# Units 3 and 4 moved between P times u and the grams, and the output turn one pair of units later

## What is computed

```python
xn = _layernorm(x, axis=-1)
x = x + _L0_attn_ref(xn, ...) + _L0_ffn_ref(xn, ...)
# attention: q, k, v through a causal convolution of 4 taps and silu, beta and g from xn
def step(S, inp):
    q_t, k_t, v_t, g_t, b_t = inp
    S = S * jnp.exp(g_t)[..., None, None]
    mem = jnp.einsum('bhk,bhkv->bhv', k_t, S)
    delta = (v_t - mem) * b_t[..., None]
    S = S + jnp.einsum('bhk,bhv->bhkv', k_t, delta)
    o_t = jnp.einsum('bhk,bhkv->bhv', q_t, S)
    return (S, o_t)
...
o = o * jax.lax.rsqrt(jnp.mean(o * o, axis=-1, keepdims=True) + eps)
o = o * jax.nn.silu(g_out.reshape(Bm, Tm, H, DV))
return o.reshape(Bm, Tm, VAL_DIM) @ o_w.T
# feed-forward, I = 1408
gate_up = jnp.einsum('bsh,oh->bso', x, w_gu)
gate, up = (gate_up[..., :I], gate_up[..., I:])
h = jax.nn.silu(gate) * up
y = jnp.einsum('bsi,hi->bsh', h, w_down)
rms = jnp.sqrt(jnp.mean(y * y, axis=-1, keepdims=True) + EPS)
return y / rms
```

## Time and profile before

| | |
|---|---|
| median of 3 runs | 3232.68 us (3232.13 to 3233.97) |
| the profiled execution | 3249.4 us, span 3247.6 us |
| PE busy, share of the span | 3114.7 us, 96% |
| DVE busy | 2489.0 us, 77% |
| POOL busy | 1912.5 us, 59% |
| ACT busy | 1664.1 us, 51% |
| DMA, mean busy share of 16 engines, stretch of the loop | 0.06 |

### The profile page before, as it was taken

How to read it: one execution, slowest core, us unless ns; L and a number is a source line. 1 busy time by engine, 2 the same in 40 slices (tenths; PEclk the granted TensorE clock), 3 DMA queues, 4 the chain that set the end, 5 groups by cost and what they waited for, 6 DMA issues and landing times.

```text
span 3247.6 us, 117622 instructions
## 1 busy us (share of the span) xinstructions
PE 3114.7 (96%) x45504; PEld 2207.2 (68%) x45504; DVE 2489.0 (77%) x5509; ACT 1664.1 (51%) x3336; POOL 1912.5 (59%) x2955
## 2 busy tenths in 40 slices
PE   5999999999999999999999999999999999999987
PEld 4676776766766766766767767667667666667664
DVE  7777777877777777777777777777777777777763
ACT  4544555544555545555445555445555455554452
POOL 4566555666555665556665556665556665566642
PEclk8999999999999999999999999999999999999997
DMA  3000000000000000000000000000000000000000
GB/s 121 8 21 19 8 18 21 21 21 15 9 21 21 21 21 5 18 22 21 21 19 8 18 21 21 21 15 9 21 21 21 21 5 18 22 21 21 15 3 21
DMA packets 34301, 64.95 MB, mean 20 GB/s; under 512 B 5360, under 2 KB 7152, under 8 KB 33776
## 3 DMA queue, kind: packets, MB, share of 16 engines
q1 hardware_dynamic: 29808, 52.13, 5.0%
q10 hardware_dynamic: 4096, 6.42, 0.6%
HBM read 41.76 MB, written 16.78 MB: 18 GB/s over the span
## 4 chain that ended last, share of the span: by engine, by line
PE 78%; DVE 14%; issue 5%; POOL 2%; ACT 0%; DVEq 0%; DMA 0%; SPq 0%; POOLq 0%; ACTq 0%
PE PS L1220 14%; PE PS L1176 14%; PE PS L1207 8%; PE PS L1208 7%; PE PS L1432 7%; PE PS L1292 6%; DVE arena L912 5%; PE PS L1275 3%; PE PS L1357 3%; DVE arena L1012 2%; PE PS L1310 2%; PE PS L1410 2%; PE PS L1328 2%; DVE arena L384 2%; PE PS L1232 1%
## 5 line engine op out<-in xcount | busy, mean ns | idle before, releaser
L912 DVE SCALAR_TENSOR_TENSOR arena<-PS,sc,arena 128x256 f32<-128x256 f32 x2112 | 1000.7, 480 | 358.6 <-ACT arena L606 236.5
L1207 PE MATMUL PS<-xh,wgu 128*128 128x256 f32 x2816 | 901.4, 352 | 15.1 <-DVE arena L912 10.6
L1208 PE MATMUL PS<-xl,wgu 128*128 128x256 f32 x2816 | 700.7, 281 | 0.0
L606 ACT ACTIVATE arena<-PS,sc 128x256 f32<-128x256 f32 x704 | 329.8, 473 | 708.0 <-PE PS L1208 704.0
L1220 PE MATMUL PS<-wdn,inner 128*128 128x512 f32 x1408 | 656.3, 592 | 0.0
L1207 PEld LDWEIGHTS PS<-xh,wgu 128*128 128x128 f32 x2816 | 530.9, 189 | 146.8 <-issue 76.3
L503 POOL TENSOR_TENSOR work<-arena 128x31 f32<-128x31 f32 (+15 forms) x992 | 521.4, 526 | 141.0 <-DVE arena L1012 65.8
L1208 PEld LDWEIGHTS PS<-xl,wgu 128*128 128x128 f32 x2816 | 531.6, 189 | 97.3 <-issue 97.1
L507 POOL TENSOR_TENSOR arena<-arena,work 128x31 f32<-128x31 f32 (+15 forms) x992 | 543.1, 547 | 77.9 <-POOL work L503 0.2
L1176 PE MATMUL PS<-xnT,wqkv 128*128 128x256 f32 x2048 | 490.2, 391 | 9.0 <-ACT inner L586 9.0
L1176 PEld LDWEIGHTS PS<-xnT,wqkv 128*128 128x128 f32 x2048 | 382.5, 193 | 75.3 <-issue 13.6
(11 more groups left out here) (160 smaller groups left out, 4665.2 us busy)
## 6 DMA issues: line engine op xcount, KB each, us to landing
xt<-in_x SPq DMA_DIRECT2D x64, 256.0 KB, 3.4
obuf<-in_x SPq DMA_DIRECT2D x64, 256.0 KB, 2.8
out<-obuf SPq DMA_DIRECT2D x64, 256.0 KB, 2.0
wqkv<-in_wqkv ACTq DMA_DIRECT2D x1, 2048.0 KB, 14.1
arena<-in_gup ACTq DMA_DIRECT2D x2, 704.0 KB, 6.4
arena<-in_dns SPq DMA_DIRECT2D x1, 1408.0 KB, 12.1
wg<-in_wg ACTq DMA_DIRECT2D x1, 1024.0 KB, 20.6
wo<-in_wo ACTq DMA_DIRECT2D x1, 1024.0 KB, 17.2
```

Source lines behind the costliest of these rows:

```text
L606: eng.activation(fa[:, u % 4, :], PS[:, bank(u, 0), 0:NB * P], ACT.Copy, scale=sc[:, u % 2, KB * m:KB * m + 1]).then_inc(fa_scaled.sem, 1)
L912: eng.scalar_tensor_tensor(out=fa[:, u % 4, :], in0=PS[:, bank(u, k // 2), k % 2 * NB * P:][:, 0:NB * P], scalar=sc[:, u % 2, KB * m + k:K ...
L1207: eng.matmul(o, w, xh[:, k, :], start=True, stop=False)
L1208: ins = eng.matmul(o, w, xl[:, k, :], start=False, stop=True)
```

## The change

On PE, units 3 and 4 and the last gate parts are written between the quarters of `p_times_u` and the two grams. Unit 5 and then the turns of v follow the second gram, and `down(0)` after them. Units up to 5 fill banks 5 and 4, where unit 4 filled 2 and 3; even units from 6 on fill 2 and 3. `turn_o` moves from behind unit 8 to behind unit 10, the four parts of `to_wo` from behind units 10 to 16 to behind units 12 to 18. ACT and DVE follow: DVE takes unit 3 and hidden(1) ahead of the reductions and unit 4 ahead of the gram products, ACT the silu of v ahead of unit 2. `result` and `layer_norm_apply` change places.

```diff
--- before.py
+++ after.py
@@ -358,7 +358,7 @@
 
         def bank(u, fill):
 
-            return 2 + fill if u >= 4 and u % 2 == 0 else 5 - fill
+            return 2 + fill if u >= 6 and u % 2 == 0 else 5 - fill
 
         def gate_bank(b):
             return 6 if b else 4
@@ -767,8 +767,13 @@
 
 
             unit(1)
+            if n:
+                eng.wait_ge(*taps_done.at(n, NQKV))
+                eng.activation(qkv[:, 4:NQKV, :], qkv[:, 4:NQKV, :], ACT.Silu).then_inc(silu_done.sem, 1)
+            unit(2)
             queries()
-            unit(2)
+            gate(1)
+            unit(3)
             if t:
                 eng.wait_ge(*pu_out.at(t, 1))
                 for b in range(NB):
@@ -786,18 +791,14 @@
                 eng.activation(ro[:, :, :], ro[:, :, :], ACT.Exp, scale=-0.5).then_inc(last_roots.sem, 1)
                 o_columns()
                 return
-            eng.wait_ge(*taps_done.at(n, NQKV))
-            eng.activation(qkv[:, 4:NQKV, :], qkv[:, 4:NQKV, :], ACT.Silu).then_inc(silu_done.sem, 1)
+            unit(4)
             gate_copy(1)
-            unit(3)
-            gate(1)
-            unit(4)
+            unit(5)
+            gate(2)
             for b in range(NB):
                 eng.wait_ge(*v_turned.at(n, b + 1))
                 eng.activation(R[:, b, :, 0:DV], PS[:, 6 + b, :].rearrange("p (h v) -> p h v", h=H),
                                ACT.Copy).then_inc(v_copied.sem, 1)
-            unit(5)
-            gate(2)
             if t:
                 eng.wait_ge(*o_gated.at(t, NB))
             eng.activation(gs[:, :, :], gsn[:, :, :], ACT.Silu).then_inc(gs_done.sem, 1)
@@ -807,7 +808,7 @@
                 unit(2 * m)
                 unit(2 * m + 1)
                 gate(m)
-                if m == 4:
+                if m == 5:
                     o_columns()
             if more:
                 x_transposed(eng, n.next(), n)
@@ -1087,6 +1088,8 @@
             unit(1)
             hidden(0)
             unit(2)
+            unit(3)
+            hidden(1)
             if t:
                 for b in range(NB):
                     eng.wait_ge(*osq_done.at(t, b + 1))
@@ -1094,10 +1097,9 @@
                                       ALU.add).then_inc(so_done.sem, 1)
                 if not n:
                     last_output()
+            unit(4)
             gram_products(0)
             gram_products(1)
-            unit(3)
-            hidden(1)
             if n:
                 turn_a(0)
             if not n:
@@ -1107,15 +1109,16 @@
 
 
             for m in range(2, FM):
-                unit(2 * m)
+                if m > 2:
+                    unit(2 * m)
                 unit(2 * m + 1)
                 hidden(m)
                 if m == 2:
                     turn_a(1)
-                if t and m in (6, 8):
-                    result((m - 6) // 2)
-                if more and m in (7, 9):
-                    layer_norm_apply(eng, n.next(), (m - 7) // 2)
+                if more and m in (6, 8):
+                    layer_norm_apply(eng, n.next(), (m - 6) // 2)
+                if t and m in (7, 9):
+                    result((m - 7) // 2)
             turn_t()
             eng.wait_ge(*res_loaded.at(n, 16 * NB))
             for i, b in enumerate((1, 0)):
@@ -1193,9 +1196,9 @@
                             eng.wait_ge(wgu_by_act.sem, 2)
                             eng.wait_ge(wgu_by_pool.sem, 2)
                             eng.wait_ge(wdn_done.sem, FM)
-                elif u <= 3:
+                elif u <= 5:
                     eng.wait_ge(*(fa_done if fill else fa_second).at(n, u))
-                elif u == 4:
+                elif u == 6:
                     if fill == 0:
                         eng.wait_ge(*p_done.at(n, NB))
                 else:
@@ -1505,20 +1508,23 @@
 
             half_unit(1, 0)
             gate(1, 0)
+            gate(1, 1)
             p_times_u(0)
             half_unit(1, 1)
             p_times_u(1)
+            half_unit(2, 0)
             turn_q()
-            gate(1, 1)
-            p_times_u(2)
-            half_unit(2, 0)
-            p_times_u(3)
             half_unit(2, 1)
             gate(1, 2)
+            p_times_u(2)
+            half_unit(3, 0)
+            p_times_u(3)
+            half_unit(3, 1)
+            gate(1, 3)
+            half_unit(4, 0)
             gram(0)
+            half_unit(4, 1)
             gram(1)
-            gate(1, 3)
-            unit(3)
             if not n:
                 turn_o()
                 for b in range(NB):
@@ -1527,23 +1533,22 @@
                 return
 
 
+            unit(5)
             for b in range(NB):
                 eng.wait_ge(*silu_done.at(n, NC + 1))
                 eng.wait_ge(*gate_copied.at(n, NB))
                 for m in range(4):
                     ins = eng.transpose(PS[:, 6 + b, m * P:(m + 1) * P], qkv[:, 4 + m, b * P:(b + 1) * P], ident[:, :])
                 ins.then_inc(v_turned.sem, 1)
-            unit(4)
-            unit(5)
             down(0)
             for i in range(6, NU):
                 unit(i)
                 if i % 2:
                     down((i - 5) // 2)
-                elif i == 8:
+                elif i == 10:
                     turn_o()
-                elif 10 <= i <= 16:
-                    to_wo((i - 10) // 4, (i - 10) // 2 % 2)
+                elif 12 <= i <= 18:
+                    to_wo((i - 12) // 4, (i - 12) // 2 % 2)
             down(9)
             if more:
                 transpose_x(eng, n.next(), t)
```

## The result

The changed kernel is slower: 3258.09 us (3253.97 to 3259.02, 4 runs) against 3233.32 (3232.13 to 3235.01, 4 runs) on one chip, ratio 1.0074, 95% interval 1.0061 to 1.0087. Forecast was 3198, faster, with a range of 3178 to 3222. The profiled execution took 3253.97 us; that of before, from which the prediction was worked, 3249.4.

A forecast was written before the change was run, and what follows sets the result against it. TensorE was taken as the bound. Fetch losses -1.39, waits -0.90-0.43, new waits +0.86+0.4, shifted starts +0.3 gave -1.1 us per iteration; with 0.15 more fetch, 31 steps gave -34, the first tile -1: 3232.7 to 3198, range 3178 to 3222.

The forecast's parts named there:

- The order on PE: From half_unit(1, 0) to the end of gram 1, the new TensorE order takes 13.74 us, bursts 0.68, half grams 1.02.
- the rows 128 apart: TensorE stops in bursts 128 rows (256 instructions) apart, awaiting instruction blocks available every 3.9 us; wide work between avoids most stops.
- The size of that term: Instruction-fetch losses at P times u and the grams: 1.55 us per iteration, nearly all expected to go, 0.15 kept.
- DVE is also held by unit 4, now ahead of them: On VectorE, unit 4 precedes the gram products; its last two steps end at 1065.2.
- So products start at 1065.25 and end at 1067.75: VectorE's gram products, which down(0) needs; TensorE, there at 1066.89, then waits 0.86 us.
- the reductions end 3.03 after the last burst: VectorE's reductions keep their old distance of 3.03 us behind the last P times u burst, so end at 1063.29.
- 0.86 at down(0): New TensorE wait of 0.86 us before down(0), for VectorE's gram products.
- 0.4 at unit 9: New TensorE wait of 0.4 us: unit 9's second half needs unit 7 done on VectorE.
- idle at unit 5: Sign of being wrong: TensorE idle at half_unit(4, 1) or unit 5, waiting on DVE.
- nothing for or against: After down(2), output turn and projection stand in pairs where DVE is level with PE: no gain or loss.
- The issue losses stay: Rival, chance 0.10: losses belong to the bursts, not to time since the last block; 3246 us, slower.
- the banks bite: Rival, chance 0.12: single banks and ScalarE's order make edges of units 3 to 5 miss, losing 0.5 us; 3214.

The follow-up runs named there:

- run 7: Kernel before with gate part 1 moved ahead of the first quarter of P times u on TensorE: 3236.22 us, ratio 1.0003.
- Run 5: Kernel before, unchanged, traced and timed again on one chip: 3235.16 us, ratio 0.9998.
- run 9: Changed kernel with one added wait: GpSimd starts its gate product only when hidden(1) is done: 3213.26 us, ratio 0.989.
- Run 1: Changed kernel with GpSimd's product of o with the gate on 8 of 512 columns only: 3229.53 us, ratio 0.9967.
- run 2: Changed kernel with hidden(1) moved behind the gram products on VectorE: 3213.9 us, ratio 0.9921.
- run 10: Kernel before with hidden(0) moved between the two reductions, inside GpSimd's first gate product: 3246.85 us, ratio 1.0002.
- run 3: Changed kernel with output turn and projection back at their old places: 3238.03 us, ratio 0.9993.
- run 8: Changed kernel with hidden(1) behind the gram products and output turn and projection at their old places: 3195.98 us, ratio 0.9874.
- run 11: Kernel before with only the output turn, projection and results one pair of units later: 3265.59 us against 3245.26, ratio 1.0062.

## Why the prediction was wrong

**The order on PE: right.** In the iteration shown all bursts take 0.68 and gram 0 1.00, and the stretch 13.6 us for 13.74. In the mean of all iterations the first burst is 0.74 and the others 0.68. The losses went as the rows 128 apart said, and run 7 shows by itself that they follow the count of rows. That a block of instructions has not landed is read from the count and from the packets of the instruction queue. The Trainium skill ("Runtime: NRT & Kernel Launch", Instruction fetch mechanics) gives blocks of 256 instructions, and the trace agrees (128 rows of two). By that page crossings are mostly hidden; in this kernel they cost 1.0 to 1.55 us an iteration.

**The size of that term: off.** The prediction took 1.55 us an iteration from one execution and subtracted it from the median of others. Run 5 puts it at 1.0. That is some 16 of the missing microseconds (15.5 to 17, run 5). The sign of it was in sight: the traced execution was 16.7 us above the median, and the prediction took that as a constant beside the sum.

**The step that failed: "DVE is also held by unit 4, now ahead of them", which led to "So products start at 1065.25 and end at 1067.75".** It took it that "the reductions end 3.03 after the last burst", as before, though hidden(1) now stands ahead of them, at the moment when GpSimd begins its gate product, and the prediction held that nothing on POOL is moved. hidden(1) took 1.47 there, and the reductions ended 4.54 us after the last burst (3.50 in run 9, where hidden(1) takes 0.43). The products started 0.9 later than forecast in the iteration, down(0) 1.0. hidden(2) met the scaling in the same way, 0.6 more, and with it down(2) was 1.4 late. Run 1 takes the first meeting away and gets 27 us, run 9 takes both away and gets 44, and run 2 comes to the same 3214 by order. 3198 forecast + 16 for the blocks + 44 for the two meetings = 3258; that it comes out to the microsecond is luck, as the 44 is a distance between chips. The forecast of the waits themselves, 0.86 at down(0) and 0.4 at unit 9, was right in place. They became 1.07 (1068.29 to 1070.18, less 0.82 for the turns) and 0.8 (4.43 from down(1) to down(2), less 3.62), and unit 5's two waits, 0.3 and 0.5, were not forecast at all; the prediction had named idle at unit 5 as a sign that it was wrong.

What happens in a meeting is seen in the rows: the product that starts second waits for the end of the one GpSimd instruction that is under way, and then takes its own time. hidden(1) began 0.09 us into an instruction of 1.27 and took 1.47, about 1.2 of waiting and 0.3 of work. hidden(2) began 0.26 into one of 1.05 and took 1.08, hidden(0) of run 10 0.56 into one of 1.28 and took 1.00: each time it ended 0.3 us after GpSimd's instruction, whatever was left of that when it began. Slower work side by side would not do that. The Trainium skill says this ("SBUF — State Buffer", SBUF: two separate sides): DVE and GpSimd share one pair of ports under "an exclusive lock, not a bandwidth split", which a DVE operation with two SBUF inputs needs against a GpSimd operation that reads SBUF. The rows agree for GpSimd's wide multiplies, also in what is spared: unit steps and gram products with an input in PSUM, and reductions with one input. They differ for its power of 32 columns, which reads SBUF too: by that sentence hidden(1) of run 2 would have waited for the rest of the 5.43 us, and it took 0.41. The measurement decides; why the power holds nothing up stays open. In the kernel before, hidden(0) and hidden(1) fell by luck on pauses or on GpSimd's powers and took 0.43; hidden(2) met the end of the scaling in 14 of 30 iterations of the first trace and took up to 0.61.

**The output turn: missed.** The prediction called its move "nothing for or against", though it worked out the 0.4 us wait at unit 9 in which the turn used to stand. Putting it back is worth some 18 us with the meetings (run 3) and again 18 without (run 8 against 2), both between chips, and moving it alone costs 20 on one chip (run 11).

**The rivals.** None was the true one. "The issue losses stay" gave 3246 on the right side for a wrong reason; "the banks bite" named the right waits, but runs 1 and 9 leave banks and order alone and the loss goes: in run 9 no wait of a unit for DVE is left in the list.

## What to carry to other kernels

Before an instruction is moved on VectorE, look at what GpSimd does at its new place: a product of two SBUF tiles waits there for the end of a wide GpSimd multiply that reads SBUF, and half a microsecond earlier or later can decide 0.65 to 1.0 us in each iteration. One semaphore that lets the short one go first was worth some 44 us of 3257. Dense runs of small matmuls want wide ones between them, and wide work is also what fills a wait of TensorE for another engine. The same piece cannot do both, so its place is chosen with both in view. And where the traced execution is slower than the median, find out which term holds the difference before that term is subtracted.

## What the runs showed of the hardware

- A DVE product of 128x256 in two SBUF tiles: 0.43 us, and 1.00, 1.08 or 1.47 when it starts inside a GpSimd multiply of 1.05 to 1.28 us. It ends 0.3 us after that multiply. The GpSimd multiply behind it is up to 0.2 us longer (2.70 for both instead of 2.51). Beside GpSimd's power of 32 columns (5.43 us) it takes 0.41 to 0.43.
- TensorE's stops in dense 32x32 matmuls stand at fixed rows: in the kernel before at row 51 of the first burst and, 128 pairs of load and matmul later, at row 41 of the third. That is 256 instructions, as in one 16 KB packet of the instruction queue. A third, in the grams, stands 126 pairs on. From the end of the first to the end of the second lie 3.6 to 3.9 us in that trace. In the changed kernel the same 128 pairs take 4.3 us, and the second stop is gone. Wide work moved ahead of one burst takes its stop away and lengthens the next (run 7).
- How long these stops are differs by execution and chip: 1.55 and 1.0 us an iteration in two traces of one kernel. The kernel before took 3233, 3236, 3241 and 3245 us in four groups of runs, the changed one, nearly without stops, 3258 and 3256 in two of them.
